# Rotation tables of the dense attention made in the first block and spread in DRAM; its norm moved into the transposes' block

## The reference

```
x = x + mamba(ctx_1024, layernorm(x))            # layer 0, attention slot
x = x + ffn_4bit(layernorm(x))                   # layer 0, ffn slot
x = x + dense_attention(layernorm(x), ctx_1024, pos, pos)   # layer 1
...
def apply_axial_rope(x, pos):                    # 32 heads of 16, p = 2 axes
    half = 4
    freqs = 10000.0 ** (-arange(half) / half)
    ang = pos[..., :, None] * freqs
    out = stack([x1 * cos(ang) - x2 * sin(ang), x1 * sin(ang) + x2 * cos(ang)])
```

## Time and profile before

| | us |
|---|---|
| median of 3 runs | 4247.79 (4243.83 to 4247.87) |
| the profiled execution, its own time | 4247.61 |
| its span in the trace | 4245.6 |

### The profile page before, as it was taken

How to read it: one execution, slowest core, us unless ns; L and a number is a source line. 1 busy time by engine, 2 the same in 40 slices (tenths; PEclk the granted TensorE clock), 3 DMA queues, 4 the chain that set the end, 5 groups by cost and what they waited for, 6 DMA issues and landing times. The chain is left out here.

```text
span 4245.6 us, 46735 instructions
## 1 busy us (share of the span) xinstructions
PE 3610.5 (85%) x15184; PEld 1723.7 (41%) x15184; DVE 2977.1 (70%) x4169; ACT 1769.3 (42%) x2947; POOL 1500.1 (35%) x1038
## 2 busy tenths in 40 slices
PE   6888846999999999698999879785886777679898
PEld 2233323555555555342333344343332322244454
DVE  4899988578877774557888256527667999844663
ACT  4555532222222221243777453336664555421254
POOL 3898954112211120054000100003445999900122
PEclk8899977999999999797999989896998999989999
DMA  4455431132133302256775110002004554412320
GB/s 124 133 136 138 131 117 39 48 99 71 62 99 101 94 27 66 84 128 107 79 77 57 53 60 0 3 0 72 0 0 134 136 139 133 130 47 69 79 54 22
DMA packets 246858, 333.98 MB, mean 79 GB/s; under 512 B 43428, under 2 KB 145062, under 8 KB 245576
## 3 DMA queue, kind: packets, MB, share of 16 engines
q1 hardware_dynamic: 246648, 331.36, 31.6%
HBM read 280.17 MB, written 51.13 MB: 78 GB/s over the span
## 5 line engine op out<-in xcount | busy, mean ns | idle before, releaser
L652 ACT ACTIVATE m_dA<-m_delta,m_a_neg 128x512 f32<-128x512 f32 x512 | 350.0, 689 | 472.5 <-DVE m_H_bank L745 384.9
L504 PE MATMUL m_y<-m_H,ident 128*128 128x512 f32 x512 | 307.4, 689 | 186.4 <-DVE m_H L762 186.4
L1833 DVE TENSOR_REDUCE a_core_minus_max<-a_core_a 128x1 f32<-128x512 f32 x512 | 317.1, 684 | 59.1 <-PE a_core_a L1659 59.1
L684 POOL TENSOR_TENSOR m_dB<-m_du,m_BC 128x1024 f32<-128x1024 f32 x128 | 315.5, 2465 | 44.4 <-DMA m_BC<-bc_ready 35.7
L512 PE MATMUL m_y<-m_H,ident 128*128 128x512 f32 x512 | 294.2, 665 | 31.1 <-POOL m_H L666 30.9
L666 POOL TENSOR_TENSOR m_H<-m_H,m_BC 128x512 f32<-128x512 f32 x224 | 299.9, 1339 | 45.5 <-DVE m_H L754 43.9
L1785 ACT ACTIVATE X<-a_core_s 128x512 f32<-128x512 f32 x512 | 264.6, 603 | 94.5 <-PE a_core_s L1659 94.5
L684 POOL TENSOR_TENSOR XN<-m_du,m_BC 128x1024 f32<-128x1024 f32 x128 | 300.8, 2356 | 2.7 <-DMA m_BC<-bc_ready 2.7
L1225 POOL TENSOR_TENSOR ctxT<-ctxT,f_scales 128x1024 f32<-128x1024 f32 x48 | 104.2, 2171 | 532.4 <-DVE ctxT L1050 532.4
L1291 DVE SCALAR_TENSOR_TENSOR XN<-f_u,f_power_back,XN 128x512 f32<-128x512 f32 x128 | 95.8, 749 | 231.0 <-PE f_u L1122 231.0
L1185 ACT ACTIVATE XN<-f_g,f_power_back 128x512 f32<-128x512 f32 x128 | 88.0, 687 | 403.6 <-PE f_g L1122 403.5
(11 more groups left out here) (411 smaller groups left out, 8395.3 us busy)
## 6 DMA issues: line engine op xcount, KB each, us to landing
m_BC<-bc_rows SPq DMA_DIRECT2D x224, 512.0 KB, 4.9
XN<-in_L_ffn_w_dram SPq DMA_DIRECT2D x72, 256.0 KB, 2.6
m_BC<-bc_ready SPq DMA_DIRECT2D x32, 512.0 KB, 4.9
ternary<-ctxT SPq DMA_DIRECT2D x96, 128.0 KB, 1.7
a_core_q<-a_q_parts SPq DMA_DIRECT2D x48, 256.0 KB, 13.0
a_core_k<-a_k_parts SPq DMA_DIRECT2D x48, 256.0 KB, 14.8
f_w_tern<-ternary SPq DMA_DIRECT2D x24, 512.0 KB, 5.9
f_core_q<-f_q_parts SPq DMA_DIRECT2D x24, 512.0 KB, 8.0
```

Of the source, the lines that this page charges most:

```text
L504: pe.matmul(ps_y[:, 0, :], ident[:], HD[n % NH], start=False, stop=True, skip_group_check=True).then_inc(s_ad, 1)
L652: act.activation(dA[:, i % NA, :], delta[b % 2][:, e, :], ACT.Exp, scale=a_neg[:, e, k % N:k % N + 1]).then_inc(s_dA, 1)
L684: pool.tensor_tensor(dB[n % ND][:], du[b % 2][:, h * EH:(h + 1) * EH, :], BC[n % NS][:, 0:1, :].broadcast_to([P, EH, L]), ALU.mult).then_i ...
L1833: dve.tensor_reduce(mx[u % 2][:, qt, h:h + 1], ps_a[:, at % NR, 0:n], AX.X, ALU.max, negate=True).then_inc(s_red, 1)
```

## The change

- `stage_start` makes a compact table, 128 rows (8 angles x 16 position tiles) by 128 positions, for sine and cosine together (128 x 2 x 128). Its SP program first waits until DVE has zeroed two tiles, then issues four new DMAs (per axis: 2048 positions picked one by one with a stride, and one row of rates to 16 partitions) **ahead of** the context's load. DVE, PE and ACT make the angles and the sine ahead of their work on the context. Behind `X`'s load SP waits for the sine, stores the table (128 KB) to DRAM, and waits until it has landed; the block ends behind that.
- `stage_ffn4`: SP issues four DRAM to DRAM DMAs that write the full tables (2 MB) from the compact one (128 KB); at the end of the block it waits for them.
- `stage_attention`: `rope_tables` is gone. `transpose_norm` gets `rows=True` and does the norm itself, as `split_norm_transposed` does. SP loads weights, then both full tables (2 MB), then parks `X`. DVE waits for the tables ahead of its first product.

The diff, cut to its core:

```diff
 def stage_start(chip, x, ctx_dram, weights, pos, freq, table):
@@ sync
+            sp.wait_ge(s_zero, 2)
+            for a in range(A):
+                sp.dma_start(prow[:, a:a + 1, 0:NT].rearrange("p o t -> p (o t)"), pos.rearrange(
+                    "b (t p) a -> a p (b t)", p=P)[a], allow_slow_non_contiguous=True).then_inc(s_pos, 16)
+                sp.dma_start(fr[a * QUAD:a * QUAD + NT, :], freq[a:a + 1, :].broadcast_to([NT, P])).then_inc(s_fr, 16)
             sp.dma_start(cn[:], ctx_dram.rearrange("b (t p) c -> p (b t) c", p=P)).then_inc(s_c, 16)
             weights.load_rows(sp)
             weights.load_small(sp)
             sp.dma_start(X[:], x.rearrange("b (t p) c -> p (b t) c", p=P)).then_inc(chip.loaded, 16)
+            sp.wait_ge(s_sin, 1)
+            sp.dma_start(table.rearrange("s q t -> q s t"), tab[:]).then_inc(s_tab, 16)
+            sp.wait_ge(s_tab, 16)
@@ tensor
             pe.wait_ge(s_id, 1)
+            pe.wait_ge(s_pos, 16 * A)
+            pe.transpose(ps_r[0:Q, 0, 0:P], prow[:].rearrange("p a t -> p (a t)"), ident[:]).then_inc(s_rt, 1)
+            pe.wait_ge(s_rc, 1)
+            pe.wait_ge(s_rate, A)
+            pe.matmul(ps_r[:, 1, 0:P], rates[:].rearrange("q r t -> q (r t)"), posT[:], start=True,
+                      stop=True).then_inc(s_ang, 1)
             pe.wait_ge(s_c, 16)
@@ scalar
+            act.wait_ge(s_red, 1)
+            act.activation(tab[:], ang[:], ACT.Sin).then_inc(s_sin, 1)
@@ vector
+            dve.memset(prow[:], 0.0).then_inc(s_zero, 1)
+            dve.memset(fr[:], 0.0).then_inc(s_zero, 1)
...
+            for i in range(2):
+                ch.did(dve.tensor_scalar(ang[:, i, :], ps_r[:, 1, 0:P], i * PI / 2, None, ALU.add))
...
+            dve.tensor_scalar(ang[:], ang[:], 3.1415925, -3.1415925, ALU.min, ALU.max).then_inc(s_red, 1)
-def transpose_norm(chip, name, xnT, preload=lambda sp: None):
+def transpose_norm(chip, name, xnT, preload=lambda sp: None, rows=False):
@@ tensor
+                if rows:
+                    pe.wait_ge((norm.s_xd, norm.s_xa)[t % 2], t // 2 + 1)
@@ scalar
+            if rows:
+                norm.root(act)
+                norm.odd_rows(act)
@@ vector
+            if rows:
+                norm.moments(dve)
+                norm.inverse(dve)
+                norm.even_rows(dve)
@@ stage_ffn4, sync
             load(sp, 1)
+            for i in range(2):
+                for o in range(2):
+                    sp.dma_start(table[i].rearrange("(h r o) n -> h r o n", h=8, o=2)[:, :, o:o + 1, :].rearrange(
+                        "h r o n -> h r (o n)"), compact[i].rearrange("(h r j) t -> h r (j t)", h=1, j=NT).broadcast_to(
+                            [8, 8, B * L])).then_inc(s_spread, 16)
             load_whole(0)
...
+            sp.wait_ge(s_spread, 64)
             sp.wait_ge(s_V, 6 * G + 2)
-def rope_tables(chip, name, pos, freq, cosT, sinT, preload):
...
@@ stage_attention
         def load_weights(sp):
-            sp.dma_start(x_dram, X[:]).then_inc(s_park, 16)
             sp.dma_start(W["q"][:], wq.rearrange("(k p) n -> p k n", p=P)).then_inc(s_w, 16)
...
+            for i, out in enumerate((sinT, cosT)):
+                sp.dma_start(out[:].rearrange("p b l -> p (b l)"), table[i]).then_inc(s_tab, 16)
+            sp.dma_start(x_dram, X[:]).then_inc(s_park, 16)
-        rope_tables(chip, name + "_rope", pos, freq, cosT, sinT, load_weights)
-        transpose_norm(chip, name + "_xnT", xnT)
+        transpose_norm(chip, name + "_xnT", xnT, load_weights, rows=True)
@@ vector
+            dve.wait_ge(s_tab, 32)
             for n, (w, b, g) in enumerate(ITEMS):
```

More of the change, by code:

```diff
@@ L113, in load_small, with stage_start @@
                          allow_slow_non_contiguous=True).then_inc(self.s_small, 16)
-def stage_start(chip, x, ctx_dram, weights):
+def stage_start(chip, x, ctx_dram, weights, pos, freq, table):
     nc = chip.nc
@@ L123, in stage_start @@
         pt = chip.ps("ctx_pt", [P, 2, 4, P], F32, st)
+        A = pos.shape[2]
+        RATES, QUAD = P // NT, 32
+        Q = A * QUAD
+        PI = float(np.pi)
+        C1 = 6.28125
+        C2 = 2 * PI - C1
+        prow, fr = chip.sb("rope_pos", [P, A, QUAD], F32, st), chip.sb("rope_freq", [Q, P], F32, st)
+        rates, posT = chip.sb("rope_rates", [Q, RATES, NT], F32, st), chip.sb("rope_posT", [Q, P], F32, st)
+        ang, turns, tab = (chip.sb("rope_" + n, [P, 2, P], F32, st) for n in ("angle", "turns", "table"))
+        ps_r = chip.ps("rope_ps", [P, 2, BANK], F32, st)
+        s_pos, s_fr = chip.sem("rope_pos"), chip.sem("rope_freq")
+        s_rt, s_rc, s_rate, s_zero = (chip.sem("rope_" + n) for n in ("turned", "posT", "rates", "zeroed"))
+        s_ang, s_ch, s_red, s_sin, s_tab = (chip.sem("rope_" + n) for n in ("angle", "chain", "reduced", "sin", "stored"))
         s_c = chip.sem("start_ctx")
@@ L166, in _ @@
         def _(dve):
+            dve.memset(prow[:], 0.0).then_inc(s_zero, 1)
+            dve.memset(fr[:], 0.0).then_inc(s_zero, 1)
             dve.wait_ge(s_id, 1)
             dve.tensor_copy(chip.identb[:], ident[:]).then_inc(s_idb, 1)
+            dve.wait_ge(s_fr, 16 * A)
+            for a in range(A):
+                rows = slice(a * QUAD, (a + 1) * QUAD)
+                dve.tensor_tensor(rates[rows], fr[rows, 0:2 * RATES].rearrange("q (r two) -> q r two", two=2)[
+                    :, :, 0:1].broadcast_to([QUAD, RATES, NT]), ident[rows, a * QUAD:a * QUAD + NT].rearrange(
+                    "q (o t) -> q o t", o=1).broadcast_to([QUAD, RATES, NT]), ALU.mult).then_inc(s_rate, 1)
+            dve.wait_ge(s_rt, 1)
+            dve.tensor_copy(posT[:], ps_r[0:Q, 0, 0:P]).then_inc(s_rc, 1)
+            ch = Chain(dve, s_ch)
+            dve.wait_ge(s_ang, 1)
+            for i in range(2):
+                ch.did(dve.tensor_scalar(ang[:, i, :], ps_r[:, 1, 0:P], i * PI / 2, None, ALU.add))
+            ch.settle()
+            ch.step(dve.tensor_scalar(turns[:], ang[:], 1 / (2 * PI), MAGIC, ALU.mult, ALU.add))
+            ch.step(dve.tensor_scalar(turns[:], turns[:], -MAGIC, None, ALU.add))
+            for c in (C1, C2):
+                ch.step(dve.scalar_tensor_tensor(out=ang[:], in0=turns[:], scalar=-c, in1=ang[:], op0=ALU.mult, op1=ALU.add))
+            dve.tensor_scalar(ang[:], ang[:], 3.1415925, -3.1415925, ALU.min, ALU.max).then_inc(s_red, 1)
 class Norm:
@@ L804, in _ @@
                 add_y(B - 1, t)
-def transpose_norm(chip, name, xnT, preload=lambda sp: None):
+def transpose_norm(chip, name, xnT, preload=lambda sp: None, rows=False):
     XN, ident = chip.XN, chip.ident
     with ExitStack() as st:
+        norm = Norm(chip, name + "_norm", st) if rows else None
         pt = chip.ps(name + "_pt", [P, 8, BANK], F32, st)
@@ L894, in _, with stage_ffn4 @@
                                          op0=ALU.mult, op1=ALU.subtract).then_inc(s_l, 1)
-def stage_ffn4(chip, name, parked, ternary, gate_w, gate_s, up_w, up_s, down_w, down_s):
+def stage_ffn4(chip, name, parked, compact, table, ternary, gate_w, gate_s, up_w, up_s, down_w, down_s):
     nc, X, XN, ctxT, ident = chip.nc, chip.X, chip.XN, chip.ctxT, chip.ident
@@ L2964, in build @@
         bc_ready = nc.dram_tensor("bc_ready", (32, L), F32).ap()
+        compact = nc.dram_tensor("rope_rows", (2, P, P), F32).ap()
+        table = nc.dram_tensor("rope_spread", (2, P, B * L), F32).ap()
         with ExitStack() as held:
             weights = ScanWeights(chip, "m0", held, *mamba_args(a, "L0"))
-            chip.run(stage_start, a["x"], a["ctx_1024"], weights)
+            chip.run(stage_start, a["x"], a["ctx_1024"], weights, a["fside_BxSx2_0"], a["freq"], compact)
             later = ScanWeights(chip, "m0_next", held, *mamba_args(a, "L3"), rows=weights)
```

67 lines of the change are left out of this document (5 added, 62 removed).

## The result

The changed kernel takes 4224.04 us (median of 5 runs, 4218.57 to 4228.03), the kernel before, run beside it, 4243.83 (5 runs, 4238.86 to 4247.87). The ratio is 0.9954, with a 95% interval of 0.9943 to 0.9966: 0.46% faster. The forecast was 4226.6 us, in a range of 4215 to 4235; against the 4247.79 us that it started from that is a gain of 21.2 us, and side by side the medians lie 19.8 us apart.

The account below looks back on a forecast made before the run. The prediction took a chain of blocks with barriers, PE bounding most of the program. Its terms gave 4245.6 - 34.0 + 12.9 + 0.1 = 4224.6 us of span, with 2.0 us over it 4226.6 us, range 4215 to 4235.

Parts of the forecast that it names:

- Attention: Attention stage without table work: last copy 24.7 us behind the first moment, a gain of 34.0 us (32.5 to 35.5).
- the twin block: First block of the 4-bit layer, the measure for attention's new block: first transposed tile 13.35 us behind the first moment.
- the second half of the transposes: Attention's second 8 tiles, whose banks copies must empty: PE's 32 pieces at 0.147 us, 4.7 us.
- The loads ahead of the context: Program start: four small loads make the context and all behind it 3.5 us later (1.8 to 6.0).
- the slower-than-before rival: Program start: picked 4-byte elements are dear, 95 ns each eating the gain, 130 ns giving 4257 us; chance 3%.
- The store behind `X`: First block ends with `X` and the store 1.0 us later; Mamba stage starts at 30.6, 12.9 us later (10.2 to 16.0).
- fully in the queue 3 us before: Program start: `X`'s load is queued 3 us ahead of the store, an argument against the 8% rival that the store needn't wait.
- The table switch: Mamba stage: the exponential needs a 1.28 us table load on ACT after the sine; cost 0, up to 0.5 us.
- The spread: 4-bit layer: four DMAs write 2.1 MB in 5.4 us at 391 GB/s, done by 689 and hidden; cost 0.
- The rival: 4-bit layer: spread on half the engines (10.8 us), then half the rate again (21.5 us), delays the absolute piece; 4232 us, 12%.
- a change of their length: Sign of failure: the later stages, which nothing in the change touches, change their length.
- "faster": Whole kernel: faster by more than 0.2% (8.5 us), below 4239.3 us; the forecast and all rivals but the dear elements, 93%.

Follow-up runs that it names:

- the paired load: Store-first kernel, with both axes' positions in one load of 2048 8-byte pieces instead of two of 2048 4-byte pieces; 4209.07 us, ratio 0.9925.
- the store first: Changed kernel with the compact table's store issued ahead of `X`'s load instead of behind it; 4212.65 us, ratio 0.9937.
- attention only: Kernel before with the changed attention stage and the old start, the table loads reading input x instead; 4207.76 us, ratio 0.9921.
- the four-times kernel: Changed kernel with three more copies of the full tables spread, 8.4 MB written instead of 2.1; 4244.93 us in one run.

## Why the prediction was right, step by step

*Attention.* Right, 34.0 us forecast, 35.1 measured. The head, 13.35 us, is that of the twin block to the hundredth. The term that was mis-sized is the second half of the transposes: I put 32 pieces at 0.147 us, 4.7 us, by their mean in the old block. The row of after shows 3.71 us (0.116 each), and ACT's seven copies took 3.64 us, 0.52 each instead of 0.59. The mean mixed two clocks, as windows of the kernel before show (window, busy us of PE, PEld, DVE, ACT and POOL, clock, DMA share, GB/s):

```profile
1798.00:1802.00 4.00, 3.50 (x17) 3.53 (x18) 0.69 (x1) 1.37 (x3) 0.00 (x0) 0.50 0.03 6
1802.00:1806.00 4.00, 4.00 (x34) 4.00 (x33) 2.77 (x4) 2.02 (x4) 0.00 (x0) 0.87 0.00 0
```

At a granted clock of 0.50 (the lower of two levels, 1.2 of 2.4 GHz) the first 17 pieces took 0.206 us each; as the clock rose, 34 took 0.118 each. In the new block PE comes to its second half at the full clock (1.00 from 1784 to 1789), behind 5 us of transposes. So a mean over a stretch in which the clock changes is no price for a stretch in which it doesn't.

*The loads ahead of the context.* 3.5 us forecast; `X` lands 4.0 us later, the context is used at 13.30 instead of 12.8, and with the store out of the way the start is 3.9 us late. The picked pieces of 4 bytes are not dear: PE uses both axes at 6.00, 3.2 us behind the second issue and 4.84 us behind the first. If the 4096 pieces lie evenly on 16 engines, 256 on each, that is an estimate of under 19 ns each, and the slower-than-before rival falls. The price sits in the issues: a rates' load behind a picked one took 1.07 and 1.49 us to issue, not the 0.38 of a positions' issue; the paired load's two rates took 0.80 each. In the kernel before, the rates' issue behind that of the positions took 0.85 us (L1907, at 1750.25); the forecast put 0.38 on it.

*The store behind `X`.* It waited, as forecast. That PE's start came at 30.68 for 30.6 is partly luck, since three errors cancel: `X` landed 0.5 us later than forecast, 0.35 us were measured for the store where 1.0 was put, and from the block's end to PE it took 1.26 instead of 1.06. The forecast also had the load "fully in the queue 3 us before" the store; the store's issue began 0.55 us behind that of `X` and was itself held for 4.06 us, and the conclusion stood even so. And the 1.3 us of the earlier trace rows are SP's wait alone; that store landed 1.6 us behind its issue. With the store first the new one took 2.1 us from issue to landing. The Trainium skill's 2 us for a DMA's fixed part, most of it the receipt (DMA: Bandwidth & Descriptors, Anatomy of one DMA, which describes the path by GpSimd, while this store is SP's), do not show as time behind `X`. That the store's receipt ran beside the end of `X` is my reading; no row shows the two apart.

*The table switch.* The load is there at 30.64 (1.28 us), and PE goes on to the projections 6.04 us behind its start, where it was 5.91: 0, as forecast. But that hangs on PE's transposes ahead of them, which run at the lower clock here and in the kernel before (granted 0.50; 1.94 and 1.80 us for the first eight). With the store first they start at a clock of 1.00 and take 1.06 us, and then DVE's diagonals, late by the table load, end last. The first row is of that kernel, the second of attention only, which starts at the same clock and has no table load:

```profile
27.55 8.80 PE L513 MATMUL m_w<-ctxT,m_in_T 128*128 128x512 f32 x16 [3.25 <-DVE m_taps L748]
```

```profile
21.94 9.42 PE L464 MATMUL m_w<-ctxT,m_in_T 128*128 128x512 f32 x16 [1.92 <-ACT m_dt_T L548]
```

That is 5.91 against 4.64 us behind PE's start: the switch costs 1.3 us there. The paired load's kernel pays it as well (5.91 us).

*The spread.* Its price on the path was right (0), the way there was not. I had it done in 5.4 us at 391 GB/s. The changed kernel's windows at that place (columns as above) show less:

```profile
699.00:701.00 2.00, 2.00 (x6) 0.73 (x5) 0.00 (x0) 0.01 (x1) 0.00 (x0) 0.50 0.73 169
...
711.00:713.00 2.00, 2.00 (x10) 1.57 (x9) 1.97 (x4) 0.00 (x0) 0.67 (x1) 1.00 0.24 90
713.00:715.00 2.00, 2.00 (x10) 1.16 (x9) 1.93 (x4) 1.25 (x3) 1.65 (x1) 1.00 0.00 0
```

2.1 MB at 213 GB/s, the rate of the four-times kernel, are 9.8 us (an estimate: packed weights and gate pieces are in flight in the same windows), and with the gate pieces behind it on the queue the DMA engines are busy until after 711. The absolute piece is issued at 705.18. In the list of DMA issues it is the middle one of three loads (their median is its own time):

```profile
XN<-in_L_ffn_w_gate_dram SPq DMA_DIRECT2D x3, 256.0 KB, 7.6
```

So it lands at 712.8. ACT's sum comes at 714.07, with no idle time in front of it:

```profile
714.07 0.62 ACT L1265 ACTIVATE XN<-XN 128x512 f32<-128x512 f32 x1
```

The piece is in time by 1.3 us. In the kernel before it landed 2.6 us behind its issue, at 692.3, 6.3 us ahead of the sum; the spread has used up 5.0 of these. The sum is 15.52 us behind its place in the earlier trace rows, and the layer's start is 15.02 behind. The other 0.5 us arise ahead of the piece, in the slot before, where PE's granted clock rises to 1.00 about 1 us later in the slot than in the kernel before; that slot's step from ACT's first activation to its cast takes 4.54 to 5.59 us in the traces with a spread and 5.07 and 5.11 us in two without, so the spread is not its cause as far as these show. The rival was much nearer than its 12% said: of its two steps the first, half the engines, is what happened, and its own estimate for that (landing by 697 in the time of before) is 0.3 us off: 712.8 less 15.5 is 697.3. Only the second, half the rate again, did not happen. The first step is the Trainium skill's rule (DMA: Bandwidth & Descriptors, Rules for kernel authors: at most as many engines as the outermost dimension allows, here 8), and the share of 0.51, with only spreads in flight, agrees with it. The sum should have gone by that rule, with 9.8 us in place of 5.4.

*The rest.* The forecast's terms give -21.0 us of span, the trace -23.4. The 0.1 in the forecast's sum has no term of its own in the text. Attention and start with their measured sizes give -34.8 + 13.0 = -21.8. What is left is +2.1 in the scans, +0.5 in the 4-bit layer and -4.1 behind attention. The first and the last lie in stages that the change does not touch, and a change of their length was named as a sign that the prediction fails. Across all twelve traces, experiments included, the scans take 513.4 to 519.1 us, and the part from the projections to the end 2430.7 to 2436.2 us, with the kernel before's at the top of that. The profiled execution of the kernel before (4247.61 us) is also 3.8 us over its median beside the changed kernel, and slower than all 28 of its later runs (4236.43 to 4246.16), while that of the changed kernel is its median. So I take these for the difference of one execution from another, and the 19.8 us between the medians for the gain. The forecast's chances add up to 95% for its "faster", where it wrote 93%. That the layout or the later start shifts them by a microsecond or two was not tried.

## What to carry to other kernels

Table work that depends on inputs alone can be moved to where the engines stand idle, but count the queue and not the arithmetic: the 128 x 256 table was free, its store behind a 4 MB load cost 9 us, and one line earlier it cost nothing. Put what a barrier waits for ahead of the large transfer that nobody waits for, and put small loads ahead of a large one, few and in as few pieces as the layout allows (both were changed at once here, and that brought 2 us). When a transfer is hidden, ask by how much: here one spread left 1.3 us to spare, and four held the layer up by 23 us. What was free can cost something once the stage in front of it is faster, as the table switch did.

## What the runs showed of the hardware

- Small loads issued behind 2 MB come late from any of the three engines tried: used at 12.29 (SP), 15.37 (ACT) and 11.87 (GpSimd), where the 2 MB land at 9.6, 9.9 and 12.2; ahead of the 2 MB they are used at 6.00. On SP and ACT the issue instruction itself takes 5.48, 4.42 and 5.72 us (a store behind `X` 4.06, against 0.51 ahead of it); on GpSimd it takes 1.37 us at most, but the data comes hardly sooner. How deep the queue in between is, the runs don't show.
- A DRAM to DRAM copy whose outermost axis is 8 runs at 0.51 of the engines and 211 to 215 GB/s written, against 391 GB/s for the load of `X`. It does not lose a further half for reading and writing DRAM.
- 2048 picked pieces of 4 bytes are used 3.2 us behind their issue, 2048 pieces of 8 bytes 2.9 us behind theirs (paired load: 0.81 to 3.74). Half the bytes in a piece did not make a load quicker.
- A table load on ACT takes 1.28 us in every row here, and the next activation follows it at once (30.64 + 1.28 = 31.92, the next at 31.94). Whether it costs anything depends on what ends last behind it: 0 in the changed kernel, 1.3 us with the store first.
